# A graph layer in one kernel: the opening rearranged over ScalarE, SyncE and GpSimd, and place numbers written in three pieces

## What is computed

```python
edge_in = concatenate([h[row], h[col], dist], axis=1)      # h: 3125 x 64
e = silu(edge_in @ eW1 + eb1)                              # 53125 x 128
e = silu(e @ eW2 + eb2)
agg = segment_sum(e, row, num_segments=3125)
out = silu(concatenate([h, agg], axis=1) @ nW1 + nb1) @ nW2 + nb2
return layernorm(x + out)                                  # h is x
```

## Time and profile before

| | |
|---|---|
| median of three runs | 633.36 us (631.66 to 633.81) |
| the profiled execution | 633.18 us, of which the span of the core is 631.4 us |
| TensorE busy | 565.6 us (90%) |
| GpSimd busy | 432.4 us (68%), of it the gathers 419.5 us |
| VectorE busy | 427.7 us (68%) |
| ScalarE busy | 363.6 us (58%) |
| DMA | 34.23 MB, mean 54 GB/s |

### The profile page before, as it was taken

The page is one execution under the profiler, slowest core; times in us unless marked ns, Lnnn a source line. Parts: engine busy times, 40 slices in busy tenths (PEclk is TensorE's granted clock), DMA queues, the critical chain, the costliest instruction groups (busy, mean ns, idle before and its releaser), DMA issues.

```text
span 631.4 us, 15748 instructions
## 1 busy us (share of the span) xinstructions
PE 565.6 (90%) x4943; PEld 483.1 (77%) x4943; DVE 427.7 (68%) x1298; ACT 363.6 (58%) x829; POOL 432.4 (68%) x465
## 2 busy tenths in 40 slices
PE   3896889899999999999999999999998888879795
PEld 3665587788887899898788987897777777769674
DVE  6866899898689768778777678677643433223346
ACT  3475266355655675766565566556556666657554
POOL 4325777567777777777777777777777777777740
PEclk9995789889989999999999899989999999999997
DMA  5301111112212212221212122211221222221211
GB/s 120 102 14 43 51 51 51 43 44 55 51 51 52 55 51 54 54 56 52 55 52 56 51 56 52 56 51 52 56 56 51 56 55 52 56 54 53 55 39 52
DMA packets 17219, 34.23 MB, mean 54 GB/s; under 512 B 8133, under 2 KB 9352, under 8 KB 17017
## 3 DMA queue, kind: packets, MB, share of 16 engines
q0 software_dynamic: 14080, 28.86, 17.2%
q1 hardware_dynamic: 2594, 3.40, 2.1%
q10 hardware_dynamic: 468, 0.96, 0.6%
HBM read 30.73 MB, written 2.40 MB: 52 GB/s over the span
## 4 chain that ended last, share of the span: by engine, by line
POOL 37%; PE 29%; issue 16%; DVE 14%; ACT 2%; DMA 1%; DVEq 1%; POOLq 0%; ACTq 0%
POOL q_rows L819 37%; PE layer_ps L832 13%; PE sort_ps L832 9%; PE seg_ps L832 5%; DVE load_hot L1362 3%; DVE col_hot L1356 1%; PE turn_ps L978 1%; DVE row_hot L1357 1%; DVE agg L1433 1%; DMA q_rows<-q_table,q_index 1%; DVE count L1213 1%; ACT p_table L592 1%; DVE hot L1418 1%; DVE count L1254 0%; DVEq L1425 0%
## 5 line engine op out<-in xcount | busy, mean ns | idle before, releaser
L819 POOL DMA_INDIRECT q_rows<-q_table,q_index x440 | 419.5, 953 | 158.4 <-issue 129.8
L659 ACT ACTIVATE e<-layer_ps 128x512 f32<-128x512 f32 x110 | 65.7, 597 | 200.6 <-PE seg_ps L832 196.0
L1433 DVE TENSOR_TENSOR agg<-agg,seg_ps 128x125 f32 x416 | 93.2, 281 | 115.2 <-PE seg_ps L832 113.8
L832 PE MATMUL layer_ps<-hotT,p_table 128*128 128x128 bf16 x1320 | 161.5, 228 | 0.2
L832 PE MATMUL layer_ps<-ident_f,q_rows 128*128 128x128 f32 x440 | 129.2, 294 | 26.6 <-DMA q_rows<-q_table,q_index 25.8
L832 PEld LDWEIGHTS layer_ps<-hotT,p_table 128*128 x1320 | 124.9, 100 | 22.6 <-issue 1.4
L832 PE MATMUL seg_ps<-hot,e 128*128 128x125 f32 x880 | 122.1, 282 | 4.4 <-DVE agg L1433 4.4
L832 PE MATMUL layer_ps<-w_sb,h 128*128 128x128 f32 x880 | 125.3, 287 | 0.0
L832 PEld LDWEIGHTS layer_ps<-w_sb,h 128*128 128x128 f32 x880 | 113.3, 198 | 4.6
L832 PEld LDWEIGHTS seg_ps<-hot,e 128*128 128x128 f32 x880 | 106.9, 192 | 6.1 <-issue 3.8
L832 PEld LDWEIGHTS layer_ps<-ident_f,q_rows 128*128 128x128 f32 x440 | 64.9, 148 | 37.6 <-DMA q_rows<-q_table,q_index 36.7
(11 more groups left out here) (209 smaller groups left out, 470.6 us busy)
## 6 DMA issues: line engine op xcount, KB each, us to landing
q_rows<-q_table,q_index POOLq DMA_INDIRECT x440
q_table<-q_in_sb SPq DMA_DIRECT2D x1, 896.0 KB
x_sb<-in_x_dram ACTq DMA_DIRECT2D x1, 700.0 KB
q_table<-q_in_sb SPq DMA_DIRECT2D x1, 504.0 KB
out_dram<-x_sb SPq DMA_DIRECT2D x2, 224.0 KB
out_dram<-x_sb SPq DMA_DIRECT2D x1, 252.0 KB
w_in<-in_edge_weight_dram SPq DMA_DIRECT2D x1, 185.9 KB
dst_i<-in_dst_dram SPq DMA_DIRECT2D x1, 185.9 KB
```

Source lines behind the costliest of these rows:

```text
L659: A.activation(e2[:, m % 2, :], e_of(m)[:], ACT.Silu).then_inc(e2_ready, 1)
L819: P.indirect_dma_start(q_rows[:, g % RING, j, :], None, q_table, bass.IndirectOffsetOnAxis(ap=q_index[:, GT * g + j:GT * g + j + 1], axis= ...
L832: return nc.tensor.matmul(o, lhsT, rhs, start=start, stop=stop, **kw)
L1433: D.tensor_tensor(o, o, seg_ps[:, j * LO:(j + 1) * LO], ALU.add).then_inc(agg_added, 1)
```

## The change

ScalarE makes `column_sel` in place of GpSimd, ahead of its loads of `w1_sb`, with a one-element copy ahead of that; x is loaded by SyncE behind chunk 0's node numbers; ScalarE clears `agg[1]` just ahead of the loop over the groups, where GpSimd cleared it in the opening; SUM writes `count` in three pieces in place of two, a fifth, two fifths and two fifths of the segments (rounded down), and `pick` waits for them one by one; and `TURN_SLOT` is 8 in place of 7.

```diff
-TURN_SLOT, SPREAD_SLOT = 7, 10
+TURN_SLOT, SPREAD_SLOT = 8, 10
...
+        def place_bounds(k):
+            n = segments(k)
+            return [0, n // 5, n * 3 // 5, n]
...
             load_nodes(*CODED[0], src_in)
+            for a, b in ROWS:
+                sp.dma_start(x_sb[a:b, :], x.rearrange("(p b) f -> p (b f)", b=WIN)[a:b, :]).then_inc(x_in, 16)
             for a, b in ROWS:
                 sp.dma_start(w_in[a:b, :], edge_weight.rearrange("(p t) o -> p (t o)", p=EP)[a:b, :]).then_inc(w_landed, 16)
...
-            act.wait_ge(ident_ready, 1)
-            for a, b in ROWS:
-                act.dma_start(x_sb[a:b, :], x.rearrange("(p b) f -> p (b f)", b=WIN)[a:b, :]).then_inc(x_in, 16)
+            act.wait_ge(fills_ready, 1)
+
+            A.activation(wc_part[0:1, 0, 0:1], ones[0:1, 0:1], ACT.Copy)
+            act.wait_ge(ident_ready, 2)
+            A.activation(column_sel[:], ident_b[0:NMAX, 0:NMAX].unsqueeze(2).to_broadcast([NMAX, NMAX, WIN]), ACT.Copy) \
+                .then_inc(column_sel_ready, 1)
...
-            act.wait_ge(fills_ready, 1)
             clear(agg[0])
...
             copy_spread(2, 0)
+            clear(agg[1])
             for m in range(GROUPS):
...
             P.memset(fills[0][0], 1.0).then_inc(fills_ready, 1)
-            pool.wait_ge(ident_ready, 2)
-            P.tensor_copy(column_sel[:], ident_b[0:NMAX, 0:NMAX].unsqueeze(2).to_broadcast([NMAX, NMAX, WIN])) \
-                .then_inc(column_sel_ready, 1)
             pool.wait_ge(fills_ready, 1)
...
-            P.memset(agg[1][:], 0.0).then_inc(agg_clear, 1)
...
-                    if t in (0, n // 2):
-                        pe.wait_ge(place_ready, 2 * k + 1 + (t > 0))
+                    if t in place_bounds(k):
+                        pe.wait_ge(place_ready, 3 * k + 1 + place_bounds(k).index(t))
...
-                    half = segments(k) // 2 * EP
-                    for a, b in ((0, half), (half, wide)):
+                    bounds = place_bounds(k)
+                    for a, b in ((t0 * EP, t1 * EP) for t0, t1 in zip(bounds, bounds[1:])):
```

## The result

The changed kernel takes 626.75 us in the median (four executions, 625.84 to 627.19) beside 633.59 us for the kernel before: a ratio of 0.9889 with a 95% interval of 0.9864 to 0.9915. Two further measurements with more executions gave 0.9905 (0.9885 to 0.9925) and 0.9894 (0.9876 to 0.9912), so the gain is 5.6 to 6.8 us by the medians. The forecast was 4.4 us and 629.0; its direction and most of its mechanism were right and its size too small by a fifth to a third.

What follows compares the result with a forecast made beforehand. A line of GpSimd gathers behind the preparation of chunks 0 and 1 bounds the kernel; 1.8 + 2.4 + 0.2 + 0.25 - 0.25 = 4.4 us saved gives 629.0 us on the medians' scale, range 626.6 to 631.4.

Steps and rivals of the forecast that it cites:

- Start of `node_f`: Opening on VectorE: with selector and clear off GpSimd, `node_f` starts at 4.8 instead of 6.62; gain 1.8 us (0.9 to 2.7).
- The conversion: Chunk 0's `node_f` on VectorE: with no clear beside it, 0.23 us in place of 2.63; gain 2.4 us.
- the clock falls in the opening: Rival, chance 0.05: TensorE idles before OFFSET, low clock covers PICK and a third of the sort; 6.5 us lost, 635.5.
- Turning later: ScalarE copies slot 8's three before waiting for the turning, so `win_t` ends later; 0.25 us lost (0 to 0.5).
- SUM in three pieces: Chunks 0 and 1: smaller first pieces let TensorE start earlier; gain 0.2 and 0.25 us, later chunks nothing.
- Later chunks are sorted beside the gathers: nothing: SUM in later chunks: no gain; the third instruction's 0.26 us on VectorE is not on the chain there.
- its best case, 627.8: Bounds of the terms alone: best gains 2.7 + 2.4 + 0.2 + 0.25 = 5.6 us, giving 627.8.
- What was hidden: ScalarE's selector (some 1.2 us) and clear of `agg[1]` (2.8 us, 1 us to spare) were to cost nothing on the chain.
- the sign that I had named for a wrong forecast: TensorE waits for `w1_sb` ahead of `q_fill(0)` in the opening.
- this rival: Rival, chance 0.11: `w1_sb` lands at 13.0 after 6.8 us, OFFSET comes 1.4 us late; 630.4.

## Why the prediction was right or wrong

**Start of `node_f`, 1.8 us: right, a little small.** It moved by 2.24 us. The memsets did run beside VectorE's constants: they last 2.44 us (1.85 to 4.29) where they took 1.92, and VectorE's constants end 0.16 us later. So the hindrance was slight. The rule of the Trainium skill that I had weighed against it (SBUF — State Buffer, section "Who interferes with whom") would have given 5.75 if it held for all of these instructions; 4.38 was measured.

**The conversion, 2.4 us: right.** The clear alone away from GpSimd turns 2.59 into 0.19, and 4.64 us of start and conversion came through to chunk 0's total and to OFFSET. At the thirteenth gather the three traces of the changed kernel are 5.05, 3.79 and 3.87 us ahead of the kernel before, where 4.4 was forecast. That this agrees so well is partly luck: the start gained 0.44 us more than I had put, and the wait of the next point, which I had not put at all, took some of it back.

**Not in the sum: ScalarE's copies.** VectorE now waits for them. In the three traces of the changed kernel it is 0.53, 0.53 and 1.47 us, though the granted clock from 18 to 22 us was 0.57, 1.00 and 0.69. Five traces with a clock of 1.00 from 17 to 28 us have 0.53 as well, so that much has another reason than the clock; waits of 0.91 to 1.47 stand only in traces with a low spell, but not in all of those. My rival "the clock falls in the opening" thus occurred in small: 4 us at a mean of 0.57 instead of PICK and a third of the sort. A price of 6.5 us is not seen; what this spell cost is not shown apart.

**"Turning later", 0.25 us lost: not seen.** Alone it gives a ratio of 0.9999, and in the changed kernel ScalarE's `win_t` follows its neighbour without waiting.

**"SUM in three pieces", 0.45 us: the step that failed.** Chunks 0 and 1, put at 0.2 and 0.25, gave nothing that can be measured alone. "Later chunks are sorted beside the gathers: nothing" was the larger error: three pieces alone gave 1.6 to 1.9 us, and one piece in the later chunks costs 2.2 in chunks 5 to 8 and 3.2 in chunks 2 to 4. Beside the gathers is not the same as off the path. A gather issued under a piece ends 0.82 us behind the piece, and behind the 138th gather every such hold stays in a line that waits for nothing else. That is 0.8 us of the gain, by the traces side by side. About 0.6 us more lies behind the last gather and has no shown cause. Over all chunks the sums beside SUM overlap, 1.8 to 2.7 us with two pieces and 1.6 to 2.4 with three, so one pair of traces would not have shown it. I had the long gathers in the trace of before, seven of them with 2.74 us over the usual in sum, in a group whose mean of 953 ns hid them.

The Trainium skill has a rule that fits this in the same section that I had cited for the memsets (SBUF — State Buffer, "Who interferes with whom"): a VectorE instruction with two inputs in SBUF contends with a GpSimd instruction that reads SBUF. The Trainium skill adds on the same page (SBUF — State Buffer, "Summary: rules for kernel authors") that the second of the two to issue blocks until the first finishes. The trace agrees with that for gathers issued under SUM, which reads `count` and `in_win`: they end 0.82 us behind the piece. That a gather's work on GpSimd counts as such a read is not shown by a run here.

**The sum.** The parts run alone give 1.6 + 2.1 + 1.7 - 0.3 = 5.1 us by the medians, the whole 5.6 to 6.8. One part of the difference is shown: with the clear alone TensorE waited 0.95 us for x, and the whole does not. The rest lies within what these measurements can tell. The forecast's range has a slip as well: its best case, 627.8, less 1 us of scatter is 626.8 and not 626.6.

**What was hidden stayed hidden.** The selector and the clear of `agg[1]` cost nothing that can be seen. `w1_sb` showed the sign that I had named for a wrong forecast, a wait of TensorE ahead of `q_fill(0)`, but at 0.34 and 0.29 us, and OFFSET did not move with it. That it stayed so small is partly luck: I had counted against this rival that the 6.8 us to landing were spent behind x, but without x ahead of them the loads still took 5.9, 5.8 and 5.3 us. They came in time because they left at 3.43, where I had put 5.5. GpSimd's waits for TensorE's first layer stayed near the 12.0 us of before (12.3, 13.3 and 11.4). The end came 6.0 us earlier in the profiled spans, of which 5.05 stand at the thirteenth gather and 5.32 at the last; the rest, 0.7, stands behind the last gather, where the traces with two and three pieces differ.

## What to carry to other kernels

Work on one engine beside a saturated line on another is free only if neither holds up the other: look at the single longest instructions of the saturated group and at what ran on the neighbours then, not at the group's mean. Here the kind of instruction decided: SUM, with both inputs in SBUF, held up gathers, and longer VectorE instructions with an input in PSUM did not. Cutting SUM from two pieces into three was worth 1.6 to 1.9 us; five pieces brought nothing more that was shown. And a start that moves earlier pulls in the next engine's order: x had to change its queue as well, and the copies on ScalarE were the next thing late.

## What the runs showed of the hardware

- A gather on GpSimd issued under SUM, a VectorE instruction with both inputs in SBUF, ends 0.82 us behind that piece's end, whether 0.24 or 1.26 us of it were left. Under a scan of 2.76 us with one input in PSUM gathers keep their 0.94 us. A gather that was under way when the piece began was not lengthened: with one piece in chunks 2 to 8 the gather of 170.01 took its 0.94 although a piece of 1.52 us began at 170.60; the next, of 171.26, took 1.69.
- ScalarE issued the transfer of `w1_sb` at 3.43, 0.01 us after the selector's start and 1.2 before its end; I had assumed that it waits for it. The table load of 1.28 us ran at 0.72, ahead of any wait, where it had stood at 5.11.
- Memsets on GpSimd beside short VectorE constants cost 0.16 us on VectorE and 0.5 on GpSimd; the conversion under the 2.71 us clear stood still for all of it.
- TensorE's pace in the opening differs between executions of one kernel. Between 18 and 22 us the granted clock averaged 0.57, 1.00 and 0.69 in the three traces of the changed kernel. In the one with 1.00, eight matmuls of `q_fill` from 12.88 took 3.75 us where they took 1.97 in the first, and the thirteenth gather stood at 59.34 instead of 58.08; so a granted clock of 1.00 does not say that TensorE runs at full pace there, and the rows here do not tell why.
